# Output stage of a two-layer gated cross-attention block: layer norm's normalising moved from VectorE to ScalarE, and the attention chunks spread one beside each tile

## The chip, the cores and the metric

The kernel runs on one core of a Trainium2 chip. The metric is the device time of one execution in microseconds. A core has five engines that run side by side and are ordered only by semaphores: TensorE (PE), VectorE (DVE), ScalarE (ACT), GpSimd (POOL) and SyncE (SP), which here issues the DMA transfers.

## The reference, cut to what matters

The program is two layers of gated cross-attention and feed-forward over 2048 tokens of 512 numbers. The change lies in the last stage, which is this part of it:

```python
def _layernorm(x, axis=-1, eps=1e-05):
    m = jnp.mean(x, axis=axis, keepdims=True)
    v = jnp.var(x, axis=axis, keepdims=True)
    return (x - m) / jnp.sqrt(v + eps)
...
x = x + jnp.tanh(g_xattn[1]) * (attn @ Wo.T + bo)
x = x + jnp.tanh(g_ffn[1]) * _L1_ffn_ref(_layernorm(x, axis=-1), ...)
# _L1_ffn_ref: gelu(h @ w1q.T + b1) @ w2q.T + b2, w1q and w2q rounded to three values
```

## The kernel before

The program has four stages, each closed by a barrier of all engines: attention of layer 0, its experts, attention of layer 1, and `l1_output_ffn`, the stage that the diff touches. Each engine has its instructions in a fixed order, written out by hand; an instruction waits for semaphores, and everything behind it on its engine waits with it.

`l1_output_ffn` first projects the attention output, adds it to the residual and takes the layer norm, for 16 tiles (`NT`) of 128 tokens, and then runs the feed-forward over 4 blocks (`NBLK`) of 512 tokens (`TPB` = 4 tiles each). The attention output comes transposed from memory (`aT`) in 16 chunks, each 128 of the 512 features by one block of 512 tokens; `KC` = 4 chunks make a block. A chunk is split for TensorE into a high part (ScalarE, `a_high_part`, L2319) and the rest (GpSimd, `a_low`, L2286), which stand in `h_hl`. The same tile `h_hl` later takes the normalised tokens. The first four chunks are split ahead of the loops over the tiles; the others "beside" tiles, as `chunks_beside(n)` says:

```python
def chunks_beside(n):
    return range(KC + 2 * n, min(KC * NBLK, KC + 2 * n + 2))
```

So tiles 0 to 5 have two chunks each. For one tile n these steps follow on each other:

- TensorE, `project_out(n)` (L2359): 12 matmuls of the attention output with Wo into `y_ps`. It waits until the chunks of its block are split (which counts at n = 4, 8 and 12) and until `add_output(n-2)` has emptied its PSUM buffer.
- VectorE, `add_output(n)`: adds the gated projection to `y` (L2451), then `bn_stats` (L2454), `bn_aggr` (L2456) and variance plus epsilon into `rstd` (L2458). It waits for GpSimd's `add_bias(n)` (L2291) and for the projection.
- GpSimd: `rstd` to the power -0.5 (L2300), then `add_bias(n+2)`, then `a_low` of the chunks beside n.
- VectorE, `normalise(n)` (L2465): (y - mean) * rstd into `hs`, 128x512.
- TensorE, `turn(n)` (L2368): four transpositions of `hs` into `y_ps`. It waits for `normalise(n)` and for `h_low_part(n-2)`.
- ScalarE, `h_high_part(n)` (L2327): the high part of the turned tile into `h_hl`, then the high parts of the chunks beside n.
- VectorE, `h_low_part(n)` (L2471): the rest of the turned tile.

TensorE's loop is `project_out(n)`, `turn(n-2)`. VectorE's loop is `add_output(n)`, `h_low_part(n-2)`, `normalise(n)`. SP loads the chunks through a ring of four buffers: chunk n waits until chunk n-4 is split. Behind the chunks on SP stand the pieces of the feed-forward's weights (L2247), which VectorE rounds (L2422, L2424): two before the tiles, the others behind all tiles. After the last turn TensorE begins the feed-forward (`hidden` L2386, `down` L2400).

Of the kernel before, what the change touches and what calls it, by code (L numbers as in the profile page):

```python
# [14 lines left out]
P = 128  # L15
# [3 lines left out]
ALU = mybir.AluOpType  # L19
ACT = mybir.ActivationFunctionType  # L20
# [9 lines left out]
def f32(ap):  # L30

    return ap.bitcast(F32)
# [2094 lines left out]
def l1_output_ffn(nc, new_sem, x2, aT, W, w_ffn, sums, out):  # L2127
# [5 lines left out]
    KC = D // P  # L2133
    NT = T // P
    NBLK = T // BLK
# [8 lines left out]
    with ExitStack() as c:  # L2144
        def sb(name, shape, dt=F32):
            return c.enter_context(nc.sbuf_tensor("f_" + name, shape, dt))

        def sem(name):
            return new_sem("f_" + name)
# [10 lines left out]
        y = sb("y", [P, NT, D])  # L2160
# [8 lines left out]
        hs = sb("hs", [P, 2, D])  # L2169
        ident = sb("ident", [P, P])  # L2170
        ones = sb("ones", [P, P])
        mhalf = sb("mhalf", [P, 1])
# [5 lines left out]
        stats = sb("stats", [P, 2, 6])  # L2178
        mv = sb("mv", [P, 2, 2])
        rstd = sb("rstd", [P, 2, 1])  # L2180

        w_neg = hs[:].rearrange("p s d -> p (s d)")

# [21 lines left out]
        ln_stats = sem("ln_stats")  # L2205
        ln_mv = sem("ln_mv")
        ln_eps = sem("ln_eps")
        ln_rstd = sem("ln_rstd")
        ln_done = sem("ln_done")
        h_turned = sem("h_turned")  # L2210
# [17 lines left out]

        def chunks_beside(n):

            return range(KC + 2 * n, min(KC * NBLK, KC + 2 * n + 2))

        block = c.enter_context(nc.Block())

# [38 lines left out]
        @block.gpsimd  # L2273
        def _(pool):
            pool.memset(ones[:], 1.0).then_inc(const_made, 1)
            pool.memset(mhalf[:], -0.5).then_inc(const_made, 1)
            pool.wait_ge(const_made, 2)
            pool.affine_select(out=ident[:], in_=ones[:], compare_op=ALU.is_equal, fill=0.0, base=0,
                               pattern=[[-1, P]], channel_multiplier=1).then_inc(const_made, 1)
            pool.sem_inc(g_split, 2)  # L2280
            pool.sem_inc(gelu_ready, 2)

            def a_low(n):
                own = slice(n // KC * BLK, (n // KC + 1) * BLK)
                pool.wait_ge(a_high, n + 1)
                pool.tensor_tensor(h_hl[:, 1, n % KC, own], a_raw[:, n % RING, :], f32(h_hl[:, 0, n % KC, own]),  # L2286
                                   ALU.subtract).then_inc(a_split, 1)

            def add_bias(n):
                pool.wait_ge(x_in[n // TPB], 16)  # L2290
                pool.tensor_tensor(y[:, n, :], y[:, n, :], tg_bo[:], ALU.add).then_inc(bo_added, 1)  # L2291

            for n in range(KC):
                a_low(n)
            pool.wait_ge(const_done, 2)
            add_bias(0)
            add_bias(1)
            for n in range(NT):
                pool.wait_ge(ln_eps, n + 1)
                pool.tensor_tensor(rstd[:, n % 2, :], rstd[:, n % 2, :], mhalf[:], ALU.pow).then_inc(ln_rstd, 1)  # L2300
                if n + 2 < NT:
                    add_bias(n + 2)
                for m in chunks_beside(n):
                    a_low(m)
            with pool.Fori(0, NBLK) as t:
                for m in range(NG * FC):
                    pool.wait_ge(g_high, NG * FC * t + m + 1)
                    pool.tensor_tensor(a_hl[:, 1, m % FC, :], act_sb[:, m % 2, :], f32(a_hl[:, 0, m % FC, :]),  # L2308
                                       ALU.subtract).then_inc(g_split, 1)

        @block.scalar
        def _(act):
            act.wait_ge(gates_in, 16)
            act.activation(tgs[:], gates[:], ACT.Tanh).then_inc(tg_ready, 1)

            def a_high_part(n):
                own = slice(n // KC * BLK, (n // KC + 1) * BLK)
                act.wait_ge(a_in[n % RING], 16 * (n // RING + 1))
                act.activation(h_hl[:, 0, n % KC, own], a_raw[:, n % RING, :], ACT.Copy).then_inc(a_high, 1)  # L2319

            for k in range(KC):
                a_high_part(k)
                act.wait_ge(wo_in[k % 2], 16 * (k // 2 + 1))
                act.activation(a_hl[:, 0, k, :], act_sb[:, k % 2, :], ACT.Copy).then_inc(wo_high, 1)
            for n in range(NT):
                act.wait_ge(h_turned, n + 1)
                act.activation(h_hl[:, 0, :, n * P:(n + 1) * P],  # L2327
                               y_ps[:, 2 + n % 2, :].rearrange("p (k n) -> p k n", k=KC), ACT.Copy).then_inc(h_high, 1)
                for m in chunks_beside(n):
                    a_high_part(m)  # L2330
            act.wait_ge(const_in, 48)
            with act.Fori(0, NBLK) as t:
                for m in range(NG * FC):
                    n = NG * FC * t + m
                    act.wait_ge(hid_ready, n + 1)
                    act.wait_ge(g_split, n + 1)
                    act.activation(act_sb[:, m % 2, :], h_ps[:, m % 2, :], ACT.Gelu, bias=b1[:, m:m + 1])\
                        .then_inc(gelu_ready, 1)
                    act.wait_ge(gelu_ready, n + 1 + 2)
                    act.activation(a_hl[:, 0, m % FC, :], act_sb[:, m % 2, :], ACT.Copy).then_inc(g_high, 1)  # L2340
# [71 lines left out]
        def _(dve):  # L2412
# [33 lines left out]
            def add_output(n):  # L2446

                s = n % 2
                dve.wait_ge(bo_added, n + 1)
                dve.wait_ge(o_ready, n + 1)  # L2450
                dve.scalar_tensor_tensor(y[:, n, :], y_ps[:, s, :], tgs[:, 0:1], y[:, n, :], ALU.mult, ALU.add)\  # L2451
                    .then_inc(o_added, 1)
                dve.wait_ge(o_added, n + 1)
                dve.bn_stats(stats[:, s, :], y[:, n, :]).then_inc(ln_stats, 1)  # L2454
                dve.wait_ge(ln_stats, n + 1)
                dve.bn_aggr(mv[:, s, :], stats[:, s, :]).then_inc(ln_mv, 1)  # L2456
                dve.wait_ge(ln_mv, n + 1)
                dve.tensor_scalar(rstd[:, s, :], mv[:, s, 1:2], LN_EPS, None, ALU.add).then_inc(ln_eps, 1)  # L2458

            def normalise(n):  # L2460
                s = n % 2
                dve.wait_ge(ln_rstd, n + 1)
                if n >= 2:
                    dve.wait_ge(h_turned, n - 1)
                dve.tensor_scalar(hs[:, s, :], y[:, n, :], mv[:, s, 0:1], rstd[:, s, :], ALU.subtract, ALU.mult)\  # L2465
                    .then_inc(ln_done, 1)

            def h_low_part(n):
                own = slice(n * P, (n + 1) * P)
                dve.wait_ge(h_high, n + 1)  # L2470
                dve.tensor_tensor(h_hl[:, 1, :, own], y_ps[:, 2 + n % 2, :].rearrange("p (k n) -> p k n", k=KC),  # L2471
                                  f32(h_hl[:, 0, :, own]), ALU.subtract).then_inc(h_split, 1)

            for n in range(NT + 2):
                if n < NT:
                    add_output(n)
                if n >= 2:
                    h_low_part(n - 2)
                if n < NT:
                    normalise(n)  # L2480

            dve.wait_ge(h_split, NT)
            dve.sem_inc(y_added, TPB)
# [12 lines left out]
def build(nc, a, out):  # L2496
# [36 lines left out]
    with nc.sbuf_tensor("place", [P, 2, T // P], I32) as place, \  # L2533
            nc.sbuf_tensor("weight", [P, 2, T // P], F32) as weight:
        stage(l0_experts, x1, part("b_"), x_shared, rows, slot_token, expert_out, place, weight)
        with nc.sbuf_tensor("magnitudes", [P, 2, D // P * a["w_ffn"].shape[0] // 2], F32) as sums:
            stage(l1_attention, x_shared, expert_out, place, weight, a["ctxT"], part("c_"), a["w_ffn"], x2, qT, kT, vT,
                  aT, sums)
            stage(l1_output_ffn, x2, aT, part("d_"), a["w_ffn"], sums, out)
# [56 lines left out]
```

## Time and profile before

| | |
|---|---|
| median of 3 runs | 2358.07 us (2353.35 to 2362.89) |
| the profiled execution | 2350.3 us |
| its span in the profile | 2348.5 us |
| mean granted TensorE clock | 0.946 of full speed |
| TensorE busy | 2119.5 us, 90% of the span |
| VectorE, ScalarE, GpSimd busy | 1051.3, 916.9, 1207.5 us |

The span is what the profiler shows from the first to the last instruction; the 1.8 us between it and the execution's own time lie around it. All times of rows are microseconds from the span's start unless they are marked ns. Names are those of the program with a letter for the stage ahead (`f_` for this one); `f_totals` is `y_ps`. A clock of 1.00 is 2.4 GHz, one of 0.50 is 1.2 GHz.

### The profile page before, as it was taken

The page shows a single profiled execution, that of the slowest core. Times are in us where ns is not written, and L with a number is a line of the kernel's source. Part 1 is how long each engine was busy: PE and PEld are TensorE (multiplying, and loading weights), DVE is VectorE, ACT ScalarE, POOL GpSimd, SP SyncE. Part 2 cuts the span into 40 slices and gives each one's busy share as a digit, 9 for nine tenths or more (in the row PEclk, how much of TensorE's full clock was granted, in tenths as well). Part 3 has the DMA queues.
Part 4 walks back from the last instruction along what each step waited for, and adds up shares of the span by engine and source line. Part 5 has one row for each costly group of instructions (what it writes and reads, how often), then busy time and mean ns, then how long its engine had stood idle before and what let it go on. Part 6 is the DMA issues. An engine that isn't in the chain of part 4 may idle for free. (4 is left out here: it accounts for less than half of the span.)

```text
span 2348.5 us, 30901 instructions
## 1 busy us (share of the span) xinstructions
PE 2119.5 (90%) x10728; PEld 1730.3 (74%) x10728; DVE 1051.3 (45%) x1582; ACT 916.9 (39%) x1709; POOL 1207.5 (51%) x861
## 2 busy tenths in 40 slices
PE   6999999999999996999899999997598875689998
PEld 5888788778878885788677777775477754468886
DVE  3556556644665475224223333333465343585110
ACT  4335334433534362212133343332267766223332
POOL 6755775477447753411666566663534322444332
PEclk9999999999999998799999999998799877799999
DMA  4222322232133313401045444444785553513000
GB/s 149 90 87 75 126 90 90 68 130 99 63 100 116 117 38 101 143 19 54 19 145 172 160 147 159 148 142 175 197 220 165 128 143 102 188 33 99 18 18 18
DMA packets 171450, 255.49 MB, mean 109 GB/s; under 512 B 45808, under 2 KB 70384, under 8 KB 169552
## 3 DMA queue, kind: packets, MB, share of 16 engines
q1 hardware_dynamic: 160048, 213.09, 29.0%
q0 software_dynamic: 8704, 25.19, 3.8%
q10 hardware_dynamic: 2592, 15.73, 1.7%
q8 instruction: 74, 1.21, 0.2%
q14 instruction: 32, 0.26, 0.0%
HBM read 200.45 MB, written 53.52 MB: 108 GB/s over the span
## 5 line engine op out<-in xcount | busy, mean ns | idle before, releaser
L1089 PE MATMUL b_gate_up<-b_h_hl,b_gu_hl 128*128 128x512 f32 (+1 forms) x1656 | 398.1, 399 | 3.9 <-POOL b_gu_hl L890 3.3
L238 POOL TENSOR_TENSOR a_w_hl<-a_w_raw,a_w_hl 128x2048 fp32r<-128x2048 f32 x65 | 299.9, 4614 | 163.3 <-ACT a_w_hl L300 163.2
L1089 PEld LDWEIGHTS b_gate_up<-b_h_hl,b_gu_hl 128*128 128x128 f32 (+1 forms) x1656 | 299.3, 182 | 89.5 <-POOL b_gu_hl L890 3.4
L901 POOL TENSOR_TENSOR b_a_hl<-b_prod,b_a_hl 128x512 fp32r<-128x512 f32 (+1 forms) x69 | 88.9, 1290 | 255.8 <-ACT b_a_hl L997 255.3
L1101 PE MATMUL b_y_sum<-b_dn_hl,b_a_hl 128*128 128x512 f32 (+1 forms) x828 | 199.1, 398 | 6.2 <-POOL b_a_hl L901 3.4
L413 PE MATMUL a_proj<-a_c_hl,a_w_hl 128*128 128x512 f32 x768 | 183.7, 399 | 20.1 <-DVE a_w_hl L530 18.1
L992 ACT ACTIVATE b_silu<-b_gate_up 128x512 f32<-128x512 f32 (+1 forms) x69 | 41.2, 597 | 392.2 <-PE b_gate_up L1089 375.0
L1101 PEld LDWEIGHTS b_y_sum<-b_dn_hl,b_a_hl 128*128 128x128 f32 (+1 forms) x828 | 159.0, 193 | 43.0 <-POOL b_a_hl L901 4.7
L300 ACT ACTIVATE a_w_hl<-a_w_raw 128x2048 fp32r<-128x2048 f32 x66 | 126.2, 1912 | 163.3 <-PE a_proj L413 106.7
L413 PEld LDWEIGHTS a_proj<-a_c_hl,a_w_hl 128*128 128x128 f32 x768 | 146.5, 193 | 52.6 <-issue 18.1
L487 PE MATMUL a_proj<-a_w_hl,a_a_hl 128*128 128x512 f32 x768 | 179.6, 392 | 3.9 <-DVE a_a_hl L586 3.9
L413 PE MATMUL a_proj<-a_w_hl,a_c_hl 128*128 128x512 f32 x768 | 181.3, 392 | 0.0
L319 ACT ACTIVATE a_sq<-a_proj,a_vecs 128x512 f32<-128x512 f32 x128 | 88.0, 690 | 230.5 <-PE a_proj L413 154.9
L413 PE MATMUL a_proj<-a_a_hl,a_w_hl 128*128 128x512 f32 x768 | 176.4, 390 | 0.0
L487 PEld LDWEIGHTS a_proj<-a_w_hl,a_a_hl 128*128 128x128 f32 x768 | 142.7, 188 | 34.4 <-POOL a_w_hl L238 5.5
L1296 DVE TENSOR_TENSOR b_prod<-b_silu,b_gate_up 128x512 f32<-128x512 f32 (+1 forms) x69 | 47.3, 686 | 269.3 <-ACT b_silu L992 245.1
L413 PEld LDWEIGHTS a_proj<-a_a_hl,a_w_hl 128*128 128x128 f32 x768 | 143.6, 188 | 29.7
L262 POOL TENSOR_TENSOR a_ssum<-a_ssum,a_sq 128x512 f32<-128x512 f32 x112 | 145.6, 1300 | 37.7 <-ACT a_sq L319 34.0
L2308 POOL TENSOR_TENSOR f_a_hl<-f_act_sb,f_a_hl 128x512 fp32r<-128x512 f32 x64 | 89.4, 1399 | 145.7 <-ACT f_a_hl L2340 145.6
L413 PEld LDWEIGHTS a_proj<-a_w_hl,a_c_hl 128*128 128x128 f32 x768 | 142.4, 188 | 28.6
L586 DVE SCALAR_TENSOR_TENSOR a_a_hl<-a_qT,a_vecs,a_a_hl 128x512 fp32r<-128x512 f32 x64 | 105.0, 1669 | 83.5 <-ACT a_a_hl L333 83.5
L2400 PE MATMUL f_totals<-f_ternary,f_a_hl 128*128 128x512 f32 x512 | 122.5, 396 | 0.0
(223 smaller groups left out, 3749.3 us busy)
## 6 DMA issues: line engine op xcount, KB each, us to landing
b_gu_raw<-in_b_gate_up SPq DMA_DIRECT2D x68, 352.0 KB
a_w_raw<-in_a_ki_w SPq DMA_DIRECT2D x18, 1024.0 KB, 5.1
a_w_raw<-in_a_vi_w SPq DMA_DIRECT2D x16, 1024.0 KB, 5.1
a_w_raw<-in_a_q_w SPq DMA_DIRECT2D x16, 1024.0 KB, 5.0
a_w_raw<-in_a_o_w SPq DMA_DIRECT2D x16, 1024.0 KB, 5.5
l_expert_out<-b_yg ACTq DMA_DIRECT2D x14, 1024.0 KB, 5.7
b_dn_raw<-in_b_down SPq DMA_DIRECT2D x34, 256.0 KB
p_w_piece<-in_w_ffn SPq DMA_DIRECT2D x32, 256.0 KB, 2.9
```

The costliest lines, as they stand in the source:

```text
L238: pool.tensor_tensor(w_hl[:, s, 1], w_raw[:, s], f32(w_hl[:, s, 0]), ALU.subtract)\
L262: pool.tensor_tensor(ssum[:], first, sq[:, n % 2, :], ALU.add).then_inc(sq_added, 1)
L300: act.activation(w_hl[:, i % 2, 0], w_raw[:, i % 2], ACT.Copy).then_inc(w_high, 1)
L319: act.activation(sq[:, n % 2, :], proj[:, j, :], ACT.Square, bias=bias)\
L413: mm = pe.matmul(proj[:, j, :], left, right, start=(k == 0 and n == 0), stop=(k == KC - 1 and n == 2))
L487: mm = pe.matmul(proj[:, j, :], a_hl[:, ap, k, j * P:(j + 1) * P], w_hl[:, i % 2, wp, k], start=(n == 0 and m == 0), stop=(n == 4 * G - 1 ...
L586: dve.scalar_tensor_tensor(a_hl[:, 1, n % 4, :], qT[:, n, :], v_b[:, n:n + 1], f32(a_hl[:, 0, n % 4, :]), ALU.add, ALU.subtract).then_inc( ...
L901: pool.tensor_tensor(a_hl[0:w, 1, f, :], prod[0:w, (NF * par + f) % 2, :], f32(a_hl[0:w, 0, f, :]), ALU.subtract).then_inc(a_split, 1)
L1089: mm = pe.matmul(gu_ps[0:w, n, part, :], gu_hl[:, s, wp, k, cols], h_hl[:, hslot, ap, k, :], start=(k == 0 and m == 0), stop=(k == KC - 1 ...
L1101: mm = pe.matmul(y_ps[:, j, :], a_hl[0:w, ap, f, j * P:(j + 1) * P], dn_hl[0:w, s, wp, f, :], start=(f == 0 and m == 0), stop=(f == NF - 1 ...
L2308: pool.tensor_tensor(a_hl[:, 1, m % FC, :], act_sb[:, m % 2, :], f32(a_hl[:, 0, m % FC, :]), ALU.subtract).then_inc(g_split, 1)
L2400: mm = pe.matmul(y_ps[:, j, :], a_hl[:, ap, f, j * P:(j + 1) * P], w_t[:, 2 * g + 1, f, :], start=(m == 0 and ap == 0), stop=(m == NG * FC ...
```

## The change

ScalarE now writes `hs` as rstd * y + shift, with one scale and one shift for each token, in place of VectorE's subtraction and multiplication. For this VectorE makes minus the mean (`neg`) and GpSimd multiplies it by `rstd` (`shift`). In ScalarE's loop `normalise(n)` stands ahead of `h_high_part(n-2)`. The chunks of tile n are split in round n+2 of ScalarE's and GpSimd's loops, and `chunks_beside` gives two to tiles 0 and 1 (chunks 4 to 7) and one to each of tiles 2 to 9 (8 to 15).

```diff
+        neg = sb("neg", [P, 2, 1])
+        shift = sb("shift", [P, 2, 1])
...
         def chunks_beside(n):
 
-            return range(KC + 2 * n, min(KC * NBLK, KC + 2 * n + 2))
+            first = KC + min(2 * n, n + 2)
+            return range(first, min(KC * NBLK, KC + min(2 * n + 2, n + 3)))
...
@@ gpsimd
-            for n in range(NT):
-                pool.wait_ge(ln_eps, n + 1)
-                pool.tensor_tensor(rstd[:, n % 2, :], rstd[:, n % 2, :], mhalf[:], ALU.pow).then_inc(ln_rstd, 1)
+            for n in range(NT + 2):
+                if n < NT:
+                    pool.wait_ge(ln_eps, 2 * n + 2)
+                    pool.tensor_tensor(rstd[:, n % 2, :], rstd[:, n % 2, :], mhalf[:], ALU.pow).then_inc(ln_pow, 1)
+                    pool.wait_ge(ln_pow, n + 1)
+                    pool.tensor_tensor(shift[:, n % 2, :], neg[:, n % 2, :], rstd[:, n % 2, :], ALU.mult)\
+                        .then_inc(ln_rstd, 1)
                 if n + 2 < NT:
                     add_bias(n + 2)
-                for m in chunks_beside(n):
-                    a_low(m)
+                if n >= 2:
+                    for m in chunks_beside(n - 2):
+                        a_low(m)
...
@@ scalar
-            for n in range(NT):
+            def normalise(n):
+                s = n % 2
+                act.wait_ge(ln_rstd, n + 1)
+                if n >= 2:
+                    act.wait_ge(h_turned, n - 1)
+                act.activation(hs[:, s, :], y[:, n, :], ACT.Identity, bias=shift[:, s, :], scale=rstd[:, s, :])\
+                    .then_inc(ln_done, 1)
+
+            def h_high_part(n):
                 act.wait_ge(h_turned, n + 1)
...
+            for n in range(NT + 2):
+                if n < NT:
+                    normalise(n)
+                if n >= 2:
+                    h_high_part(n - 2)
...
@@ vector
+                if n >= 2:
+                    dve.wait_ge(ln_done, n - 1)
+                dve.tensor_scalar(neg[:, s, :], mv[:, s, 0:1], -1.0, None, ALU.mult).then_inc(ln_eps, 1)
                 dve.tensor_scalar(rstd[:, s, :], mv[:, s, 1:2], LN_EPS, None, ALU.add).then_inc(ln_eps, 1)
-
-            def normalise(n):
-                s = n % 2
-                dve.wait_ge(ln_rstd, n + 1)
-                if n >= 2:
-                    dve.wait_ge(h_turned, n - 1)
-                dve.tensor_scalar(hs[:, s, :], y[:, n, :], mv[:, s, 0:1], rstd[:, s, :], ALU.subtract, ALU.mult)\
-                    .then_inc(ln_done, 1)
...
                 if n >= 2:
                     h_low_part(n - 2)
-                if n < NT:
-                    normalise(n)
```

## Rows read from the trace of the kernel before

**Rows 1.** The chain of waits in order of time: start, us, what.

```profile
2051.88 0.67 PE f_totals L2368 x4
...
2053.76 2.52 POOL f_h_hl L2286 x2
2056.29 0.52 POOL f_rstd L2300
...
2058.36 0.67 PE f_totals L2368 x4
```

**Rows 2.** Windows: us, busy (instructions) of PE, PEld, DVE, ACT, POOL, clock, DMA.

```profile
2065.00:2099.00 34.00, 27.46 (x122) 19.26 (x122) 32.47 (x55) 5.39 (x9) 13.78 (x16) 0.97 0.00 0
```

**Rows 3.** Timeline of tile 8's round, and `add_output(12)`.

```profile
2068.68 0.74 DVE L2451 SCALAR_TENSOR_TENSOR f_y<-f_totals,f_tgs,f_y 128x512 f32<-128x512 f32 x1
...
2069.50 0.60 ACT L2327 ACTIVATE f_h_hl<-f_totals 128x512 fp32r<-128x512 f32 x1 [3.35 <-PE f_totals L2368]
...
2070.47 0.68 DVE L2471 TENSOR_TENSOR f_h_hl<-f_totals,f_h_hl 128x512 fp32r<-128x512 f32 x1
2070.63 0.55 POOL L2300 TENSOR_TENSOR f_rstd<-f_rstd,f_mhalf 128x1 f32<-128x1 f32 x1 [2.15 <-DVE f_rstd L2458]
...
2071.21 1.51 DVE L2465 TENSOR_SCALAR f_hs<-f_y,f_mv,f_rstd 128x512 f32<-128x512 f32 x1
...
2084.54 0.74 DVE L2451 SCALAR_TENSOR_TENSOR f_y<-f_totals,f_tgs,f_y 128x512 f32<-128x512 f32 x1
```

**Rows 4.** Timeline of the last tiles.

```profile
2095.01 0.55 DVE L2465 TENSOR_SCALAR f_hs<-f_y,f_mv,f_rstd 128x512 f32<-128x512 f32 x1
...
2098.61 1.11 PE L2368 MATMUL f_totals<-f_ident,f_hs 128*128 128x128 f32 x4 [2.35 <-DVE f_hs L2465]
```

**Rows 5.** Timeline: two small independent operations of VectorE.

```profile
2004.57 0.17 DVE L2435 TENSOR_SCALAR f_thr<-f_mean 128x2 f32<-128x2 f32 x1
2004.65 0.16 DVE L2436 TENSOR_SCALAR f_thr<-f_mean 128x2 f32<-128x2 f32 x1
```

**Rows 6.** Groups by line and shape, GpSimd: count | busy us, mean ns | idle before.

```profile
L238 POOL TENSOR_TENSOR a_w_hl<-a_w_raw,a_w_hl 128x2048 fp32r<-128x2048 f32 x65 | 299.9, 4614 | 163.3 <-ACT a_w_hl L300 163.2
L243 POOL TENSOR_TENSOR a_c_hl<-a_c_raw,a_c_hl 128x512 fp32r<-128x512 f32 x20 | 25.5, 1275 | 8.1 <-ACT a_c_hl L304 8.1
L2300 POOL TENSOR_TENSOR f_rstd<-f_rstd,f_mhalf 128x1 f32<-128x1 f32 x16 | 8.8, 551 | 20.5 <-DVE f_rstd L2458 20.5
L266 POOL TENSOR_TENSOR a_rq<-a_rq,a_mhalf 128x4 f32<-128x4 f32 x4 | 4.1, 1024 | 18.5 <-DVE a_rq L570 18.5
L2276 POOL MEMSET f_mhalf<- 128x1 f32 x1 | 0.1, 99 | 0.0
```

**Rows 7.** Groups by line and shape, ScalarE.

```profile
L333 ACT ACTIVATE a_a_hl<-a_qT,a_vecs 128x512 fp32r<-128x512 f32 x64 | 46.0, 718 | 44.6 <-PE a_proj L487 44.6
L2319 ACT ACTIVATE f_h_hl<-f_a_raw 128x512 fp32r<-128x512 f32 x16 | 9.4, 624 | 1.4 <-DMA f_a_raw<-l_aT 1.3
L1795 ACT ACTIVATE p_outs<-p_proj,p_bias 128x512 f32<-128x512 f32 x32 | 30.4, 952 | 45.8 <-PE p_proj L1938 38.6 <-DMA p_v_b<-in_c_bv 7.2
```

**Rows 8.** Timeline of the first tiles.

```profile
2017.20 5.27 PE L2359 MATMUL f_totals<-f_a_hl,f_h_hl 128*128 128x512 f32 x12 [8.66 <-DVE f_y L2451]
2022.66 3.05 PE L2359 MATMUL f_totals<-f_a_hl,f_h_hl 128*128 128x512 f32 x12
2029.72 0.60 ACT L2327 ACTIVATE f_h_hl<-f_totals 128x512 fp32r<-128x512 f32 x1 [5.14 <-PE f_totals L2368]
2030.21 1.14 ACT L2319 ACTIVATE f_h_hl<-f_a_raw 128x512 fp32r<-128x512 f32 x2
2033.45 5.49 PE L2359 MATMUL f_totals<-f_a_hl,f_h_hl 128*128 128x512 f32 x12 [3.77 <-POOL f_h_hl L2286]
...
2045.25 0.74 DVE L2451 SCALAR_TENSOR_TENSOR f_y<-f_totals,f_tgs,f_y 128x512 f32<-128x512 f32 x1
```

**Rows 9.** Window around the second of these two groups.

```profile
2033.40:2039.00 5.60, 5.55 (x14) 4.28 (x15) 3.78 (x6) 0.00 (x0) 1.74 (x2) 0.50 0.84 247
```

More of the change, by code:

```diff
@@ L2207, in l1_output_ffn @@
         ln_eps = sem("ln_eps")
+        ln_pow = sem("ln_pow")
         ln_rstd = sem("ln_rstd")
```

## The prediction

> **What bounds the kernel now.** I read the page first, for where the time that ends last lies, then the chain of waits in order of time, then the timeline of the stage that the change touches, and last its windows. The page says that TensorE is busy 90% of the span; the chain, which the page sums by line, shows pieces of VectorE, ScalarE and GpSimd in the output stage: there something other than TensorE sets the pace. Its sixteen tiles of 128 tokens run from the first `add_output`, some 0.9 ahead of the group at 2017.20 that it releases [rows 8], to the last turn (transposition) at 2098.61 [rows 4]; from there TensorE runs the feed-forward without a stop. Only these 82 us can move.
>
> They have two paces. Up to tile 7 a tile takes 6.49 us, and the chain shows why [rows 1]: turn of a tile (2051.88, the next at 2058.36), ScalarE's `h_high_part`, its chunk's high part, two `a_low` on GpSimd (2.53 us together), GpSimd's `pow`, which is queued behind them, the normalising on VectorE, the next turn. From tile 8 there are no chunks and a tile takes 3.96 us: VectorE is busy 32.5 of 34.0 us, TensorE 27.5 [rows 2]. One such tile is in [rows 3]: `add_output` at 2068.68, `h_low_part`, `normalise` at 2071.21; `add_output(12)` at 2084.54 is four tiles of 3.96 on. `normalise` lasts 1.50 us beside GpSimd's `add_bias` and 0.55 at tiles 14 and 15, which have no `add_bias` beside them [rows 3, 4]. TensorE needs 3.05 + 0.66 and 0.16 between them, 3.87, hardly less than VectorE's loop.
>
> **The change part by part.** Call S(n) the start of `add_output(n)`.
>
> *Removed from VectorE:* 16 `normalise`, 1.50 each. *Added to it:* 16 operations of 128x1 (`neg`). A pair of such independent small operations starts 0.08 apart [rows 5], so `ln_eps` is 0.08 later: GpSimd's `pow` starts at S+2.03, not S+1.95 [rows 3].
>
> *Added to GpSimd:* a 128x1 multiply behind a wait for its own `pow`. The trace has none. Upper bound 0.55, the `pow` of the same shape [rows 6]. Lower bound 0.10, a 128x1 memset [rows 6]. Between: `pow` on 4 columns is 1.024 and on 1 is 0.551, so 0.39 is not work on columns; but subtractions of 2048 and 512 columns, 4.614 and 1.275, leave only 0.16 [rows 6]. I take 0.25, nearer the two-input arithmetic, plus 0.06 of hand-off.
>
> *Added to ScalarE:* 16 Identity activations, 128x512, with scale and bias read per partition. Copy from the same memory is 0.624, Identity with one such operand 0.718 [rows 7]; each costs 0.094, so two make 0.81. Lower bound 0.72 (the second is free), upper bound 0.95, the slowest Identity group of that size [rows 7].
>
> Of this move a row says that VectorE alone does the operation in 0.55 [rows 4]. The Trainium skill, "ScalarE: Activation LUTs", section "Rules for kernel authors", says to keep additions and multiplications on VectorE, which speaks against the edit: by it each tile pays 0.81 − 0.55 = 0.26, 4 us in sixteen. The trace here has 1.50 in fourteen of them, because of GpSimd, so by the rows the operation itself becomes shorter by 0.69.
>
> *What the order does with it.* This decides. On ScalarE, `normalise(n)` is placed ahead of `h_high_part(n-2)`. Behind that waiting instruction stand `h_high_part(n-2)` and a chunk; for `h_high_part(n-2)` waits VectorE's `h_low_part(n-2)`; and behind that stands `add_output(n+1)`. Before, `h_high_part` ran as soon as its turn was done, under VectorE's statistics (2069.50 in [rows 3]). Now a loop closes over three engines:
> S+2.03 `pow`, +0.55 = 2.58; hand-off 0.06 and multiply 0.25 = 2.89; hand-off 0.04 and Identity 0.81 = 3.74; `h_high_part` (0.60, overlapping its predecessor by 0.11 as the two instructions of ScalarE at 2029.72 and 2030.21 do [rows 8]) = 4.23; hand-off 0.03 and `h_low_part` 0.68 = 4.94; the next `add_output` overlaps it by 0.08 = 4.86.
> So a tile takes 4.86, against 6.49 with chunks before and 3.96 without. TensorE's 3.87 fits under it, and so does GpSimd (0.55 + 0.25 + 1.28 + 1.27 = 3.35).
>
> *The chunks.* Tiles 0 and 1 keep two, tiles 2 to 9 have one, and the chunks of tile m are now worked in round m+2 of ScalarE's and GpSimd's loops over the tiles. `project_out` of tiles 4, 8 and 12 needs chunks 7, 11 and 15; these were made in rounds 1, 3 and 5 and are now made in rounds 3, 7 and 11, that is in the very round before. In such a round n the chunk's high part ends 0.52 after `h_high_part`, S+4.75, and its `a_low` at 4.75 + 0.05 + 1.27 = S+6.07. Only then does `project_out(n+1)` start. TensorE has been idle some 8 us by then (ahead of tile 8 from 52.7, the end of turn 5, to 61.2). After 8.66 and 3.77 us of idle such a group took 5.27 and 5.49 us in place of 3.05 (granted clock 0.50, the 1.2 GHz level, in the second) [rows 8, 9]; I take 5.4. So S(n+1) = S(n) + 6.07 + 0.10 + 5.4 = S + 11.6: three times.
>
> *The sum of starts* (minus 2000): S(0) 16.3 unchanged. S(1) 18.2 (no `normalise` between). S(2) 22.5, set by `project_out(2)`, 17.2 + 5.3 [rows 8]. S(3) 27.4. In round 3 the `pow` waits for `a_low(5)` until 29.8, Identity ends 31.5, two chunks end 35.05, `project_out(4)` ends 40.5 = S(4); before it was 45.25 [rows 8], so the first tiles gain 4.7. Then 3 × 4.86 + 11.6 = 26.2: S(8) 66.7 (before 68.68 [rows 3]). Again: S(12) 92.8 (before 84.54 [rows 3]). Then 3 × 4.86: S(15) 107.4. The last turn needs `h_low_part(13)`, S+4.94, and starts at 112.4. Before it was 98.61 [rows 4]: **+13.8 us**. The same recurrence with the old order gives 98.3 for the kernel before, so it is good to about 0.3; I take +14.
>
> *Costed at nothing.* The wait of `neg` for `normalise(n-2)`: that ended about a tile earlier. SP's queue: chunk n waits for `a_low(n-4)`, so 11 is issued at 35 and needed at 59, 15 at 61 and needed at 85. Behind 15 stand weight pieces 2 and 3, which are now issued at 61 and are first needed when the last turn is done, at 112: the rounds between hide them. The feed-forward follows as it did. Before, TensorE came to it from an idle time of 2.35 us [rows 4], now it comes from 4 us; I cost the difference at nothing, since a group at the low clock loses no more than 2.4 us and (a) leaves room for it.
>
> A row shows VectorE's `normalise` at 1.50 where GpSimd works and 0.55 where it doesn't. The Trainium skill, "SBUF — State Buffer", section "SBUF: two separate sides", says that the two share a port pair which one instruction holds alone. By it the small operations of tile 3 would wait for `a_low(5)`: 0.4 us once, with the row before agreeing about the lock.
>
> **The rivals.**
> (a) *The small operation is dear, or the clock stays low longer.* At 0.55 the loop is 5.16 and the delay 18 us; one more slow group behind each stall also gives 18. Both bounds up (0.55 and 0.95): 20 us, 2378. For it: the `pow` rows. Against: the subtraction rows.
> (b) *Both cheap* (0.10 and 0.72): loop 4.62, +10.7, 2369, inside half a per cent.
> (c) *The clock isn't lost in the stalls.* Then each of the three slow groups is 3.05, not 5.4, and they give back 7 us: +7, 2365. Against it are both groups after long idle; for it, only that groups right behind another ran at 3.05 [rows 8].
> (d) *Faster: TensorE sets the pace.* VectorE's work falls to 0.75 + 0.73 + 0.21 + 0.24 + 0.68 = 2.6 us a tile, so by the sums of each engine TensorE's 3.87 is the bound. From S(4) = 40.5, 11 × 3.87 + 4.9 ends at 88.0: −10.6, about 2347. It decides if ScalarE's `h_high_part(n-2)` is done before `normalise(n)` and chunks come a tile before `project_out` asks; from a loop under 3.96 it begins to win. The listing's order speaks against it.
>
> **How the numbers follow.** The profiled execution took 2350.3 us (span 2348.5 and 1.8 around it), 0.33% under the median of 2358.07. With +14: 2364 for a profile, and 2372 against the median, +0.59%. Chances: forecast 0.58 (its own range 2368 to 2377), (a) 0.17, (b) 0.10, (c) 0.10, (d) 0.05. Half a per cent is 11.8 us, about what this measurement can tell from no change. The forecast lies just beyond it, so 0.08 of its chance counts as no change: slower 0.66, same 0.29, faster 0.05. The range runs from 2362, which is (c) less the 3 us that a median can be off, to 2379, just past (a)'s bound; it leaves out (d) and a little on either side.
>
> **What would show it.** Right: `add_output` starts 4.9 apart, and three gaps of about 11 to 13 ahead of tiles 4, 8 and 12, with TensorE idle some 8 us before each and its group at 5.4 after; ScalarE's `h_high_part` starting just where `normalise` ends; `normalise` at 0.8 on ScalarE; the last turn at 2112. Wrong: gaps that are missing, because a chunk was ready; a multiply far from 0.25, which moves the end by 0.14 for each 0.01; slow groups outside the three places.

## The result: about 8 to 11 us slower

The changed kernel took 2366.45 us (median of 10 runs) against 2358.0 for the kernel before: ratio 1.0034, 95% interval 1.0020 to 1.0048. A second timing of the same kernel, told below, gave 1.0045 (1.0030 to 1.0061). The forecast was 2372 in a range of 2362 to 2379, +0.59%, on the slower side. The direction and the places were right; the size was a little too large. Both ratios stay just under the half per cent that I had set as the bound of "slower", so the outcome to which I had given 0.66 did not come; by my own bound it is "no change", to which I had given 0.29.

The profiled executions differ by more, 2362.2 us of span against 2348.5, but 2.3 us of that lie ahead of the first `add_output`, which now starts at 2018.63, where the stage itself started later. So I count from there. From the first `add_output` to the start of the last turn the changed kernel needs 94.62 us, the kernel before 82.31, up to the turn at 2098.61 [rows 4]: +12.3. The first group of the feed-forward then takes 8.36 in place of 9.36: 11.3 us in all, 1.0048. The medians differ by 8.5 us in the first timing and by 10.5 in the second.

One tile of the changed kernel, tile 4, in its timeline. It begins with the turn of tile 2 on TensorE and `add_output(4)` on VectorE:

```profile
2042.08 0.60 PE L2391 MATMUL f_totals<-f_ident,f_hs 128*128 128x128 f32 x4
...
2042.35 0.75 DVE L2474 SCALAR_TENSOR_TENSOR f_y<-f_totals,f_tgs,f_y 128x512 f32<-128x512 f32 x1 [7.41 <-PE f_totals L2382]
...
2044.38 0.55 POOL L2305 TENSOR_TENSOR f_rstd<-f_rstd,f_mhalf 128x1 f32<-128x1 f32 x1 [7.07 <-DVE f_rstd L2484]
2045.00 0.19 POOL L2307 TENSOR_TENSOR f_shift<-f_neg,f_rstd 128x1 f32<-128x1 f32 x1
...
2045.23 0.82 ACT L2339 ACTIVATE f_hs<-f_y,f_shift,f_rstd 128x512 f32<-128x512 f32 x1 [9.97 <-POOL f_shift L2307]
...
2045.95 0.58 ACT L2344 ACTIVATE f_h_hl<-f_totals 128x512 fp32r<-128x512 f32 x1
...
2046.56 0.69 DVE L2489 TENSOR_TENSOR f_h_hl<-f_totals,f_h_hl 128x512 fp32r<-128x512 f32 x1 [2.27 <-ACT f_h_hl L2344]
...
2047.17 0.74 DVE L2474 SCALAR_TENSOR_TENSOR f_y<-f_totals,f_tgs,f_y 128x512 f32<-128x512 f32 x1
```

This is the loop over three engines. The turn whose result `h_high_part(2)` splits at 2045.95 had ended at 2042.68; for 3.3 us its result waited on ScalarE behind `normalise(4)`. VectorE stood idle 2.27 us for `h_high_part(2)` and began the next `add_output` 4.82 after the last one. The kernel before has no such wait: there ScalarE's part started at 2069.50, while VectorE was still at the statistics of its tile [rows 3].

TensorE in the same stretch of the changed kernel, with its idle times in brackets:

```profile
2037.36 4.88 PE L2382 MATMUL f_totals<-f_a_hl,f_h_hl 128*128 128x512 f32 x12 [8.93 <-POOL f_h_hl L2290]
...
2062.86 5.49 PE L2382 MATMUL f_totals<-f_a_hl,f_h_hl 128*128 128x512 f32 x12 [10.03 <-POOL f_h_hl L2290]
...
2088.97 4.71 PE L2382 MATMUL f_totals<-f_a_hl,f_h_hl 128*128 128x512 f32 x12 [10.03 <-POOL f_h_hl L2290]
...
2108.45 1.09 PE L2391 MATMUL f_totals<-f_ident,f_hs 128*128 128x128 f32 x4 [4.18 <-DVE f_h_hl L2489]
2113.25 1.09 PE L2391 MATMUL f_totals<-f_ident,f_hs 128*128 128x128 f32 x4 [3.71 <-DVE f_h_hl L2489]
```

These are the projections of tiles 4, 8 and 12, each held for 9 to 10 us by GpSimd's `a_low`, and each long afterwards. The windows of the second one, idle and then the group (columns as in [rows 2]), and before them a stretch without a stall:

```profile
2042.30:2052.80 10.50, 10.25 (x52) 8.01 (x50) 5.68 (x14) 3.64 (x6) 6.13 (x8) 1.00 0.19 65
2052.90:2062.80 9.90, 0.00 (x0) 0.00 (x0) 4.08 (x11) 3.63 (x6) 6.74 (x9) 0.61 0.21 53
2062.90:2068.00 5.10, 5.10 (x12) 3.99 (x13) 0.00 (x0) 0.00 (x0) 0.00 (x0) 0.50 0.73 218
```

The granted clock is 1.00, falls during the idle stretch, and is 0.50 (1.2 GHz) for the whole group that all others wait for. The chain of waits shows what that group waited for, from the round of tile 7:

```profile
2059.65 0.81 ACT f_hs L2339
2060.46 0.48 ACT f_h_hl L2344
2060.95 0.53 ACT f_h_hl L2328
2061.47 0.07 issue
2061.54 1.27 POOL f_h_hl L2290
2062.86 5.50 PE f_totals L2382 x12
```

The new operations, as groups of the stretch from 2010 to 2120:

```profile
L2339 ACT ACTIVATE f_hs<-f_y,f_shift,f_rstd 128x512 f32<-128x512 f32 x16 | 13.0, 816 | 80.2 <-POOL f_shift L2307 80.2
...
L2307 POOL TENSOR_TENSOR f_shift<-f_neg,f_rstd 128x1 f32<-128x1 f32 x16 | 3.1, 191 | 1.3
...
L2483 DVE TENSOR_SCALAR f_neg<-f_mv 128x1 f32<-128x1 f32 x16 | 2.5, 154 | 0.8 <-DVE f_mv L2479 0.3
```

### The profile page after: what moved, and what is told of

The parts are those of the page before. It is cut to its first block and busy times, and to the rows that moved or that the text cites. A ratio compares the mean times of both kernels' runs of the same rounds, so it can differ in the third digit from the quotient of the medians.

```text
span 2362.2 us, 30948 instructions
## 1 busy us (share of the span) xinstructions
PE 2116.3 (90%) x10728; PEld 1732.7 (73%) x10728; DVE 1035.7 (44%) x1582; ACT 929.4 (39%) x1725; POOL 1208.2 (51%) x877
## 5 line engine op out<-in xcount | busy, mean ns | idle before, releaser
L586 DVE SCALAR_TENSOR_TENSOR a_a_hl<-a_qT,a_vecs,a_a_hl 128x512 fp32r<-128x512 f32 x64 | 105.0, 1670 | 83.5 <-ACT a_a_hl L333 83.5
```

Of the source, the lines that this page charges most:

```text
L586: dve.scalar_tensor_tensor(a_hl[:, 1, n % 4, :], qT[:, n, :], v_b[:, n:n + 1], f32(a_hl[:, 0, n % 4, :]), ALU.add, ALU.subtract).then_inc( ...
```

## The experiments

All ratios are to the kernel before, on the same chip. "Tiles" is the time from the first `add_output` to the start of the last turn in the profile; a step is the distance of the starts of two `add_output`.

| kernel | ratio (95%) | tiles | steps |
|---|---|---|---|
| before | 1 | 82.3 | 4.0, 8.3, 6.8, 9.9 up to tile 4; then 6.49, later 3.96 |
| changed | 1.0034 (1.0020 to 1.0048) | 94.6 | 4.8; 12.7, 11.7, 10.9 ahead of tiles 4, 8, 12 |
| changed, again | 1.0045 (1.0030 to 1.0061) | 94.6 | the same |
| high part first | 0.9977 (0.9966 to 0.9987) | 77.3 | 3.24; 13.4, 10.9, 10.8 |
| chunks in their own round | 0.9983 (0.9971 to 0.9995) | 77.2 | 4.8; 8.0 ahead of tile 3 |
| both of these | 0.9883 (0.9864 to 0.9902) | 53.9 | 3.24; 4.9 ahead of tile 4, 3.4 ahead of tiles 8 and 12 |
| both, two chunks a tile | 0.9900 (0.9876 to 0.9924) | 57.6 | 4.5, then 3.24 |
| before + one chunk a tile | 1.0011 (0.9997 to 1.0026) | 83.6 | 5.25; 7.4 and 7.6 ahead of tiles 4 and 8; later 3.96 |
| changed, two chunks a tile | 1.0006 (0.9989 to 1.0022) | 83.5 | 4.8 to 5.2; 12.7 ahead of tile 4 |
| multiply twice | 1.0049 (1.0031 to 1.0067) | 98.4 | 5.08; 12.7, 11.5, 11.8 |
| before, chunks ahead of the high part | 0.9920 (0.9894 to 0.9946) | 64.5 | 4.0, then 4.44, later 3.96 |
| idle time filled | 1.0040 (1.0026 to 1.0054) | 90.3 | 4.8; 11.0, 10.8, 9.3 |

**The high part first.** The changed kernel with ScalarE's two steps exchanged (the high parts of the chunks stand inside `h_high_part` and move with it):

```diff
             for n in range(NT + 2):
-                if n < NT:
-                    normalise(n)
                 if n >= 2:
                     h_high_part(n - 2)
+                if n < NT:
+                    normalise(n)
```

> The changed kernel, with ScalarE's h_high_part(n-2) put back ahead of normalise(n); the chunks stay where they are. My theory (two separate costs: the loop over three engines, and chunks that come in the round before their projection): the loop opens, a tile takes 3.85 us (TensorE's pace) in place of 4.81, and the three stalls stay. From the first add_output to the last turn 81.5 us, against 94.6 in the changed kernel and 82.3 in the kernel before: about 13 us under the changed one, ratio to before about 1.000 (0.997 to 1.002). Rival (the loop is not what paces it; the whole loss is the three stalls): tiles stay at 4.8 us, 94 us, ratio 1.004.

The loop opened, and the three stalls stayed: steps of 3.24 between them, 17.3 us less than the changed kernel. The rival is refuted. My own number, 81.5, was too high for the measured 77.3, mainly because I had TensorE's pace as 3.85. Two tiles of its timeline show what it is:

```profile
2040.32 0.60 PE L2391 MATMUL f_totals<-f_ident,f_hs 128*128 128x128 f32 x4
2040.68 3.04 PE L2382 MATMUL f_totals<-f_a_hl,f_h_hl 128*128 128x512 f32 x12
2043.56 0.60 PE L2391 MATMUL f_totals<-f_ident,f_hs 128*128 128x128 f32 x4
```

A turn starts 2.88 after a projection that "takes" 3.04, and the next projection 0.36 after a turn of 0.60: the shown durations overlap. The pace is the distance of the starts, 2043.56 − 2040.32 = 3.24.

**Chunks in their own round.** The changed kernel with the chunks of tile n split in round n:

```diff
@@ gpsimd
-                if n >= 2:
-                    for m in chunks_beside(n - 2):
-                        a_low(m)
+                for m in chunks_beside(n):
+                    a_low(m)
@@ scalar: out of h_high_part, at the end of the round
+                for m in chunks_beside(n):
+                    a_high_part(m)
```

> The changed kernel, with the chunks of tile n split in round n and not n+2, on ScalarE and GpSimd; ScalarE's order stays normalise, h_high_part. My theory: the stalls of 11.5 us before tiles 8 and 12 vanish, the loop of 4.8 us stays; all starts from tile 4 on lie 4.8 apart. From the first add_output to the last turn 76.7 us, 18 less than the changed kernel and 5.6 less than the kernel before: ratio to before 0.9975. Rival (TensorE's low clock and not the late chunk makes the stall): the gaps shrink by no more than the 2.3 us each that a group at the low clock loses, 88 us, ratio 1.002.

The step ahead of tile 4 is 5.03 and all later ones are 4.80 to 4.81: the stalls of tiles 8 and 12 are gone, the loop stands. 77.2 us were measured where 76.7 were expected. The step ahead of tile 3 is 8.0, which I had not named: with two chunks in the round, VectorE waits 5.4 us there for `h_high_part`, which stands behind `normalise(3)`. Most of each stall was the wait for the chunk, and not the clock alone.

**Both.** The two edits together, ScalarE's round being high part, chunks, `normalise`:

> Both repairs: chunks in their own round and h_high_part(n-2) ahead of normalise(n) on ScalarE. My theory: TensorE sets the pace at 3.85 us a tile from the third tile to the last, without a stall. From the first add_output to the last turn 60 us, 22 less than the kernel before, ratio 0.9905, and the granted clock near 1.00 in this stretch. Rival (GpSimd, with bias, pow, multiply and a chunk, or the transfer of chunk 8 onward, becomes the next bound): 4.5 to 5 us a tile up to tile 11, 70 to 75 us, ratio 0.995.

Two rounds of its timeline, with the `pow` of GpSimd, and a window over nine tiles:

```profile
2049.33 0.60 PE L2390 MATMUL f_totals<-f_ident,f_hs 128*128 128x128 f32 x4
2049.60 0.75 DVE L2473 SCALAR_TENSOR_TENSOR f_y<-f_totals,f_tgs,f_y 128x512 f32<-128x512 f32 x1 [0.36 <-PE f_totals L2381]
2049.64 0.55 POOL L2305 TENSOR_TENSOR f_rstd<-f_rstd,f_mhalf 128x1 f32<-128x1 f32 x1
...
2050.50 0.82 ACT L2338 ACTIVATE f_hs<-f_y,f_shift,f_rstd 128x512 f32<-128x512 f32 x1 [1.46 <-POOL f_shift L2307]
...
2052.57 0.60 PE L2390 MATMUL f_totals<-f_ident,f_hs 128*128 128x128 f32 x4
2052.84 0.75 DVE L2473 SCALAR_TENSOR_TENSOR f_y<-f_totals,f_tgs,f_y 128x512 f32<-128x512 f32 x1 [0.32 <-PE f_totals L2381]
...
2052.92 0.55 POOL L2305 TENSOR_TENSOR f_rstd<-f_rstd,f_mhalf 128x1 f32<-128x1 f32 x1
```

```profile
2030.00:2060.00 30.00, 29.90 (x146) 24.33 (x147) 21.80 (x53) 16.27 (x27) 29.22 (x39) 1.00 0.40 122
```

TensorE is busy 29.9 of 30 us at the full clock and now ends VectorE's waits. This is the fastest version: 2323.04 us against 2351.23 beside it, 28 us less, where I expected 22; most of the 6 us more is again TensorE's real pace. The rival was nearer than it looks. GpSimd is busy 29.2 of 30 us and, while there is a chunk in each round, starts one `pow` every 3.28 us without idling (2049.64, 2052.92), hardly more than TensorE's 3.24. TensorE runs ahead by 0.04 a tile and loses it again at the next block: the steps ahead of tiles 8 and 12 are 3.36 and 3.37. So in these rounds GpSimd is already the bound, by a little; what is added to it there should cost time at once, which no run tested.

**Each half alone.** First one chunk a tile in the kernel before (only `chunks_beside` as in the diff):

> The kernel before with one half of the change, chunks_beside alone: normalise stays on VectorE, chunks stay in their own round, but only one beside each tile from tile 2 to 9. My theory: a tile with one chunk takes 5.2 us in place of 6.5 with two, for 8 tiles in place of 6, so that the sum is nearly unchanged: 82.9 us from the first add_output to the last turn against 82.3, ratio 1.000. Rival (spreading the chunks is what costs, whatever engine normalises): 90 us or more, ratio 1.003 or more.

Then the changed kernel with `chunks_beside` as it was before:

> The other half of the change alone: normalise on ScalarE with the order and the late rounds (chunks of tile n in round n+2) as changed, but two chunks beside each of tiles 0 to 5 as in the kernel before. My theory: chunks 11 and 15 are now split in rounds 5 and 7, well ahead of tiles 8 and 12, so those two stalls vanish and the one before tile 4 stays; the loop over three engines stays at 4.8, 5.2 with two chunks in it. From the first add_output to the last turn 82.9 us, ratio to before 1.000. With one chunk beside each tile but normalise on VectorE it was 83.6, so neither half costs anything and the two together cost 12: they meet in the late chunk. Rival (normalise on ScalarE costs in itself, 0.85 us a tile in sixteen tiles): 90 us or more, ratio 1.004.

Tiles took 83.6 and 83.5 us, and neither ratio can be told from 1. So the 12 us belong to neither half. But each half alone already makes TensorE wait for a chunk at tile 8 (a row of each version):

```profile
2056.44 4.62 PE L2360 MATMUL f_totals<-f_a_hl,f_h_hl 128*128 128x512 f32 x12 [2.54 <-POOL f_h_hl L2287]
2052.11 4.61 PE L2381 MATMUL f_totals<-f_a_hl,f_h_hl 128*128 128x512 f32 x12 [1.65 <-POOL f_h_hl L2289]
```

With only the chunks spread (first line) TensorE idled 2.54 us for chunk 11 and, at tile 12, 2.55 for chunk 15; the first made a step of 7.6 out of 5.25, the second was hidden under a step of 5.25. With the late rounds and two chunks a tile (second line) it idled 1.65 us at tile 8, inside a step of 5.24 like its neighbours, and not at all at tile 12. Together the two waits are 10.03 each, and nothing hides them.

**The multiply twice.** The changed kernel with GpSimd's small product computed again behind a wait:

```diff
                     pool.tensor_tensor(shift[:, n % 2, :], neg[:, n % 2, :], rstd[:, n % 2, :], ALU.mult)\
-                        .then_inc(ln_rstd, 1)
+                        .then_inc(ln_twice, 1)
+                    pool.wait_ge(ln_twice, n + 1)
+                    pool.tensor_tensor(shift[:, n % 2, :], neg[:, n % 2, :], rstd[:, n % 2, :], ALU.mult)\
+                        .then_inc(ln_rstd, 1)
```

> The changed kernel with GpSimd's 128x1 multiply done twice, each waiting for the one before. My theory (the chain add_output, pow, multiply, normalise, h_high_part, h_low_part, next add_output paces the tiles): each tile is longer by the whole of one multiply and its hand-off, 0.19 + 0.06 = 0.25, so 5.06 in place of 4.81 and 98 us from the first add_output to the last turn, in place of 94.6. Rival (GpSimd and ScalarE have slack, the pace is set by the projection): 4.81 and 94.6, unchanged.

```profile
2045.66 0.19 POOL L2308 TENSOR_TENSOR f_shift<-f_neg,f_rstd 128x1 f32<-128x1 f32 x1
2045.92 0.19 POOL L2311 TENSOR_TENSOR f_shift<-f_neg,f_rstd 128x1 f32<-128x1 f32 x1
```

The second starts 0.26 after the first, and the step went from 4.81 to 5.08: what is added to this chain is paid in full, although GpSimd idles about 1.5 us in such a tile. That shows the loop directly.

**The kernel before, with one exchange of order.** No part of the change; ScalarE splits a tile's chunks ahead of the high part of the turn:

```diff
             for n in range(NT):
+                for m in chunks_beside(n):
+                    a_high_part(m)
                 act.wait_ge(h_turned, n + 1)
...
-                for m in chunks_beside(n):
-                    a_high_part(m)
```

> The kernel before with no part of the change and one edit of order: in ScalarE's loop the high parts of the chunks beside tile n stand ahead of h_high_part(n), not behind it, so they don't wait for the turn. My theory (the 6.49 us of the first tiles come from the chunks waiting behind a turn, which waits for a pow that is queued behind those chunks): a tile with two chunks takes 4.2 us and the others 3.96 as before; 63 us from the first add_output to the last turn, in place of 82.3, ratio 0.992. Rival (GpSimd's own work of two chunks, bias and pow, 4.4 us, or the arrival of the chunks holds the first tiles): 6 us a tile stay for tiles 4 to 7, 78 us, ratio 0.998.

Two chunks a tile now cost 4.44 and not 6.49, and the longer steps up to tile 4 are gone as well: of the 17.8 us saved, 11.6 lie ahead of tile 4. I had expected 4.2 us a tile and 63 in all; 64.5 were measured. In the timeline GpSimd goes from chunk to `pow` without idling, so its own sum for two chunks, the 4.4 that the rival had named, is what bounds these tiles, and VectorE follows it:

```profile
2040.40 2.70 POOL L2286 TENSOR_TENSOR f_h_hl<-f_a_raw,f_h_hl 128x512 fp32r<-128x512 f32 x2
...
2043.07 0.55 POOL L2300 TENSOR_TENSOR f_rstd<-f_rstd,f_mhalf 128x1 f32<-128x1 f32 x1
2043.59 1.27 POOL L2291 TENSOR_TENSOR f_y<-f_y,f_tg_bo 128x512 f32<-128x512 f32 x1
2043.65 1.49 DVE L2465 TENSOR_SCALAR f_hs<-f_y,f_mv,f_rstd 128x512 f32<-128x512 f32 x1 [0.54 <-POOL f_rstd L2300]
```

So of the 28 us that the best version gains over the kernel before, 18 can be had by an exchange of two lines and nothing else. Of the other 10.6, the version with two chunks a tile at the end of this section shows 6.9 (57.6 us for 64.5) with `normalise` on ScalarE: VectorE is freed, and its step of 3.96 becomes TensorE's 3.24. The last 3.7 came with the spread of the chunks.

**The idle time filled.** The changed kernel with matmuls of no use ahead of the projections of tiles 4, 8 and 12, so that only the clock changes:

```diff
             for n in range(NT + 2):
+                if n in (4, 8, 12):
+                    for _ in range(36):
+                        pe.matmul(h_ps[:, 0, :], a_hl[:, 0, 1, 0:P], a_hl[:, 0, 0, :], start=True, stop=True)
                 if n < NT:
                     project_out(n)
```

> The changed kernel with 36 more matmuls of 128x512 (into a PSUM buffer that nothing reads) ahead of the projections of tiles 4, 8 and 12, where TensorE otherwise idles 8.9 to 10 us. At 0.216 each they take 7.8 us and end before the awaited chunk. My theory (part of each stall is the low clock after the idle time): the three groups that took 4.88, 5.49 and 4.71 take 3.05 at a granted clock of 1.00, so the gaps shrink from 12.7, 11.7 and 10.9 to about 10.8, 9.3 and 9.2; 89 us from the first add_output to the last turn in place of 94.6. Rival (those groups are long for another reason, such as operands that come late, or the clock falls anyhow): gaps unchanged, 94.6.

```profile
2031.80 8.43 PE L2397 MATMUL f_hidden<-f_a_hl 128*128 128x512 f32 x36
2041.08 3.06 PE L2382 MATMUL f_totals<-f_a_hl,f_h_hl 128*128 128x512 f32 x12 [0.85 <-POOL f_h_hl L2290]
...
2054.48 8.45 PE L2397 MATMUL f_hidden<-f_a_hl 128*128 128x512 f32 x36
2064.76 4.62 PE L2382 MATMUL f_totals<-f_a_hl,f_h_hl 128*128 128x512 f32 x12 [1.83 <-POOL f_h_hl L2290]
...
2079.73 8.44 PE L2397 MATMUL f_hidden<-f_a_hl 128*128 128x512 f32 x36
2090.00 3.07 PE L2382 MATMUL f_totals<-f_a_hl,f_h_hl 128*128 128x512 f32 x12 [1.84 <-POOL f_h_hl L2290]
```

The gaps ahead of tiles 4 and 12 shrank by 1.7 and 1.6 us, their groups taking 3.06 and 3.07. The second did not: after 8.45 us of filling and 1.83 of idle time its group took 4.62, so its gap fell by 0.9 only. The third, after 8.44 us of filling and 1.84 of idle time, took 3.07; why these two differ no run shows. The tiles took 90.3 us where I expected 89. The low clock is thus part of a stall, some 2 us of each; the other 4 to 6 are the wait. In the ratio, 1.0040, the 4.3 us can't be told: its interval overlaps both timings of the changed kernel.

**The changed kernel again.**

> The changed kernel itself, in more rounds. The traces of the two kernels give a difference of 12.3 us from the first add_output to the last turn, less 1.0 us in the feed-forward's first group, 11.3 in all or 1.0048; the first timing gave 1.0034 (1.002 to 1.0048). My theory (the tiles' times are fixed by the order, the rest is how the low clock and the early stages fall out in one execution): ratio between 1.0035 and 1.0048, and again 4.8 us a tile, three gaps of 10.9 to 12.7, 94 to 95 us to the last turn. Rival (the profiled execution overstates the loss, the stalls are shorter in others): 1.0025 or less, and gaps that differ by over 1 us from 12.7, 11.7 and 10.9.

1.0045. The three gaps were 12.68, 11.67 and 10.89 again, to the hundredth, and the tiles 94.55 us. The profile does not overstate the loss by much: the 11.3 us of the traces (1.0048) lie inside the second interval and at the upper end of the first, and both differences of medians, 8.5 and 10.5, are smaller.

**Both repairs, two chunks a tile.** It asks whether spreading the chunks pays once the order is right:

> The version with both repairs (chunks in their own round, h_high_part ahead of normalise on ScalarE), but two chunks beside each of tiles 0 to 5 as in the kernel before. It asks whether spreading the chunks is worth anything once the order is right. My theory: GpSimd then needs 4.4 us a tile while there are two chunks (pow 0.55, multiply 0.19, bias 1.28, two chunks 2.5), more than TensorE's 3.24, and TensorE catches up afterwards only in part: 57 us from the first add_output to the last turn in place of 53.9, ratio 0.9895 against 0.988. Rival (the projections run ahead, so the slower tiles are hidden): 54 us and no difference.

57.6 against 53.9 us: steps of 4.5 for the tiles with two chunks, GpSimd's own sum. By the trace the spread is worth 3.7 us; the two ratios' intervals overlap.

## Why the prediction held, point by point

*The loop over three engines* was the step on which all rested, and it is shown: 4.81 measured for 4.86, opened by one exchange (3.24) and lengthened by what was put on it (0.27 for 0.26). The multiply was 0.191 for my 0.25, between subtraction's intercept and `pow`'s; Identity with two operands per partition 0.816 for 0.81. The 0.06 that I had too much for the multiply is about the 0.05 between 4.86 and 4.81.

*The late chunks*: the stalls came ahead of tiles 4, 8 and 12. I had 13.1, 11.6 and 11.6, measured were 12.7, 11.7 and 10.9. The term that was mis-sized is the group at the low clock, 5.4 each: it took 4.88, 5.49 and 4.71, because the clock was back before the end of two of the three (mean granted clock 0.59 over 2037.30 to 2042.30, 0.50 in the second group, 0.64 over 2089 to 2094). That is 1.1 us of the 1.5 by which +13.8 was too large against +12.3; the nine ordinary steps between the stalls, 0.05 each, are the rest. TensorE idled 8.9, 10.0 and 10.0 us ahead of these groups where I had some 8: turn 5 ended 10.5 us after `add_output(4)` began, and by my too slow pace for TensorE it would have been 12.2. That cost nothing, since the chunk set the start of the group.

*The feed-forward* I costed at no difference. It gave 1.0 us back (8.36 for 9.36). The mean granted clock over this group was 0.76 in the kernel before (2099.38 to 2108.93) and 0.85 in the changed one (2113.99 to 2122.53): in the changed kernel the clock had fallen one turn earlier (0.50 already over the turn at 2108.45) and was back at 1.00 sooner in the group. With this the measured difference is +11.3 where I said +14, and the ratio fell under the half per cent instead of just above: the larger chance, 0.66 for slower, went to the wrong side of a bound that lies within 1 us of the traces. On which side of so near a bound the result fell was luck.

*The first tiles*: gained 4.7 us by the forecast; S(4) − S(0) is 23.7 against 28.95 before, 5.2.

*The shared port.* By the rule of the Trainium skill's "SBUF — State Buffer", section "SBUF: two separate sides", I had named 0.4 us at tile 3, outside the sum. The row of that `neg` in the changed kernel, and below it a `neg` of the version "high part first":

```profile
2031.61 0.15 DVE L2483 TENSOR_SCALAR f_neg<-f_mv 128x1 f32<-128x1 f32 x1 [0.25 <-DVE f_mv L2479]
...
2048.80 0.15 DVE L2483 TENSOR_SCALAR f_neg<-f_mv 128x1 f32<-128x1 f32 x1
```

The first began 0.25 late, the only one of sixteen that did with its input ready, and it ran while GpSimd's second `a_low` was still under way until 2032.11. The second ran in the middle of an `a_low` (2047.89 to 2049.16) without any delay. So these small operations are not held until GpSimd's operation ends, and the trace doesn't agree with my use of the rule: that section of the Trainium skill states the lock for VectorE operations in a two-port mode or with two inputs from SBUF, and that `neg` is one of them was my assumption. What the 0.25 was, no run shows. The delay cost nothing, since `pow` had to wait for that `a_low` anyhow.

*Rivals.* (a), the dear multiply, fell at 0.191. (b) was nearest in size, +10.7 for +11.3, but for another reason. (c) was wrong about the clock: the groups were long in all three stalls. (d) had the wrong price: with both of its conditions met the kernel gained 28 us and not 10.6. Some 7 us of this are the pace, because I had added up shown durations (3.05 + 0.66 + 0.16) where the starts are 3.24 apart. Some 10 are the first tiles: I had left the stall ahead of tile 4 in, S(4) − S(0) at 24.2, and without it 14.3 were measured. In the forecast itself the wrong pace cost nothing, since TensorE was not the bound there; it did mislead the expectations of two experiments by 4 and 6 us.

## What to carry to other kernels

On engines with a fixed order, where an operation stands in the queue can cost more than which engine runs it: here the same move was part of a loss of 11 us in one order and of a gain of 28 in another. Before moving it, write down for each engine what stands behind the new wait and who waits for that, and follow it until it closes into a loop or ends. When work is made later by k rounds, check its consumer's round as well: two edits that each cost hardly anything can meet there. TensorE's pace is read from the distance of two starts, not from a sum of durations.

## What the runs showed of the hardware

- TensorE's clock can fall after a short idle time, and need not. In the version "idle time filled" one group began 1.83 us after 8.45 us of dense matmuls at a granted clock of 1.00. It ran at 1.00 for its first 0.6 us, then at 0.50, and its twelve matmuls took 4.62 us in place of 3.05. Another group began 1.84 us after 8.44 us of the same matmuls, ran at 1.00 throughout and took 3.07; after 0.85 us of idle time one took 3.06. In the version "changed, two chunks a tile" a group after 1.65 us of idle time took 4.61.
- A small two-input operation on GpSimd (128x1 multiply) takes 0.191 us, a third of a `pow` of the same shape (0.551).
- VectorE's 128x1 operation of 0.15 us ran beside a GpSimd subtraction of 128x512 (2047.89 to 2049.16) without delay, while VectorE's 128x512 normalising took 1.50 us beside GpSimd's `add_bias` and 0.55 without it [rows 3, 4].
